# Four GNN layers on one core: the ring's first gathers put ahead of the rest pass, half steps spread over all chunks in the second layer, 28 low blocks instead of 24 in the wide layer

## What is computed

```python
x = layernorm(x + gru(x, segment_sum(mlp([x[src], edge_attr]), dst)))         # L0
x = layernorm(x + relu(conv_both_directions(x) @ W.T + bias))                 # L1: edges and reversed edges
x = layernorm(x + prelu(conv(x @ W) + b))                                     # L2: edges
h = relu(conv_w(x @ W1) + b1)      # 128 -> 256                               # L3, with edge weights
h = relu(conv_w(h @ W2) + b2)      # 256 -> 256
x = layernorm(x + conv_w(h @ W3) + b3)                                        # 256 -> 128
# conv(h)[d] = sum over edges (s, d) of norm(s, d) * h[s], and the node itself
```

## Time and profile before

| | us |
|---|---|
| median of 3 runs | 4691.67 |
| lowest, highest | 4690.04, 4700.65 |
| the profiled execution: own time | 4686.37 |
| its span, first to last instruction | 4684.6 |

### The profile page before, as it was taken

The page is one execution under the profiler, slowest core; times in us unless marked ns, Lnnn a source line. Parts: engine busy times, 40 slices in busy tenths (PEclk is TensorE's granted clock), DMA queues, the critical chain, the costliest instruction groups (busy, mean ns, idle before and its releaser), DMA issues. The chain is left out here.

```text
span 4684.6 us, 82764 instructions
## 1 busy us (share of the span) xinstructions
PE 3824.4 (82%) x30767; PEld 2562.3 (55%) x30767; DVE 3060.0 (65%) x6135; ACT 1471.8 (31%) x3024; POOL 2818.3 (60%) x2361
## 2 busy tenths in 40 slices
PE   2788899999899823277779788699989989997998
PEld 2666788888788823233334444444554555554444
DVE  5898999999999858645553334356536666633665
ACT  0333565665666602100000000033314444421332
POOL 3567788888888500067740577377727666524774
PEclk6777999998999956688999899899999999998999
DMA  5344777777777721199986677599956555545997
GB/s 162 113 126 125 222 240 228 242 237 231 248 236 237 231 92 39 48 314 317 313 262 192 201 222 228 184 323 322 330 190 207 193 183 200 183 161 206 331 327 259
DMA packets 611991, 1019.31 MB, mean 218 GB/s; under 512 B 90372, under 2 KB 417056, under 8 KB 611208
## 3 DMA queue, kind: packets, MB, share of 16 engines
q1 hardware_dynamic: 475788, 773.72, 48.5%
q0 software_dynamic: 90848, 199.74, 14.5%
q10 hardware_dynamic: 44956, 40.55, 2.7%
HBM read 736.98 MB, written 276.75 MB: 216 GB/s over the span
## 5 line engine op out<-in xcount | busy, mean ns | idle before, releaser
L871 POOL DMA_INDIRECT x<-p_table,src_i x832 | 1210.0, 1454 | 395.8 <-issue 226.3
L1373 POOL DMA_INDIRECT rows_b<-x_table,low_src x552 | 589.9, 1069 | 213.3 <-issue 165.1
L1373 POOL DMA_INDIRECT rows_a<-h_table,low_src x412 | 446.5, 1084 | 236.0 <-issue 121.1
L853 ACT CAST st_cnt<-ps_mat 128x512 bf16<-128x512 f32 (+1 forms) x825 | 440.8, 590 | 444.5 <-PE ps_deg L768 396.4
L1443 PE MATMUL po_l3b<-mat_l3b,rows_b 128*128 128x512 f32 (+1 forms) x1372 | 562.8, 557 | 20.5 <-DMA mat_l3b<-weights_fwd 19.5
L1443 PE MATMUL po_l3a<-mat_l3a,rows_a 128*128 128x512 f32 (+1 forms) x882 | 376.5, 574 | 23.5 <-DMA mat_l3a<-weights_fwd 22.7
L1443 PE MATMUL po_l3c<-mat_l3c,rows_a 128*128 128x512 f32 (+1 forms) x882 | 375.1, 572 | 16.2 <-DMA mat_l3c<-weights_fwd 15.4
L1443 PE MATMUL po_l<-mat_l,rows_a 128*128 128x512 bf16 (+1 forms) x1323 | 303.3, 384 | 87.8 <-DVE mat_l L1682 86.9
L783 PE MATMUL ps_mat<-rows_a,hot_s 128*128 128x128 bf16 x4851 | 363.5, 227 | 8.6
L1443 PEld LDWEIGHTS po_l3b<-mat_l3b,rows_b 128*128 128x128 f32 x1372 | 239.1, 194 | 237.9 <-issue 216.5
L598 DVE TENSOR_TENSOR rows_a<-rows_a,slots 128x1792 bf16<-128x1792 bf16 (+1 forms) x198 | 366.6, 1884 | 1.4
(11 more groups left out here) (407 smaller groups left out, 7663.0 us busy)
## 6 DMA issues: line engine op xcount, KB each, us to landing
weights_fwd<-st_wt SPq DMA_DIRECT2D x396, 256.0 KB
mat_l<-counts_fwd SPq DMA_DIRECT2D x112, 896.0 KB
mat_l3a<-weights_fwd SPq DMA_DIRECT2D x56, 1792.0 KB
mat_l3c<-weights_fwd SPq DMA_DIRECT2D x56, 1792.0 KB
counts_rev<-st_cnt SPq DMA_DIRECT2D x588, 128.0 KB
rev_l<-counts_rev SPq DMA_DIRECT2D x84, 896.0 KB
mat_l3b<-weights_fwd SPq DMA_DIRECT2D x42, 1792.0 KB
counts_fwd<-st_cnt SPq DMA_DIRECT2D x396, 128.0 KB
```

Source lines behind the costliest of these rows:

```text
L853: nc.scalar.copy(st_cnt[:, q, :, j * 2 * P:j * 2 * P + n_col], ps_mat[:, f % 3, :].rearrange("p (d c) -> p d c", d=2)[:, :, 0:n_col]).then ...
L871: pool.indirect_dma_start(ring[:, j % RING, t * FD:(t + 1) * FD], None, p_table, bass.IndirectOffsetOnAxis(src_i[:, j * TH + t:j * TH + t ...
L1373: pool.indirect_dma_start(ring[:, j % RL, t, :], None, table, bass.IndirectOffsetOnAxis(low_src[:, j * TH + t:j * TH + t + 1].bitcast(U32), 0)
```

## The change

1. On POOL the gathers of the first RL half steps (16 DMAs, 12 in l3b) stand ahead of the rest pass, in all five layers.
2. In l2 `usable` takes in all chunks, so the 69 half steps run to the last chunk.
3. LOWS is (16, 28): in l3b one dense group (4 blocks) becomes low. 6 dense groups and 120 half steps stand where 7 and 103 stood; 4 half steps in each of the chunks 7 to 36, where 2 or 3 stood in each of the chunks 7 to 43.
4. For room, `diag` has one buffer: `own_rows(f)` waits for `summed` f instead of f - 1. The tiles `hot2`, `edge1` and `row1` of L0's rest pass lie in the room of `x`.

```diff
-LOWS = (16, 24)
+LOWS = (16, 28)
...
-                hot2 = sb("hot2", [P, 3, P], F32, c2)
-                edge1 = sb("edge1", [ED + 1, P], F32, c2)
-                row1 = sb("row1", [P, FD], F32, c2)
+                hot2 = x_room[:, 0:3 * P].rearrange("p (q c) -> p q c", q=3)
+                edge1 = x_room[0:ED + 1, 3 * P:4 * P]
+                row1 = x_room[:, 4 * P:5 * P]
...
-            usable = sum(weights) - (0 if both else (CHKS - LATER[0] + 1) * weights[-1])
+            usable = sum(weights) - (0 if both or kind == "prelu" else (CHKS - LATER[0] + 1) * weights[-1])
...
-                diag = sb(f"diag_{name}", [P, 2, GB, P], F32, c)
+                diag = sb(f"diag_{name}", [P, GB, P], F32, c)
...
+                        def rest():
+                            rounds, tiles = rest_counts(pool)
...
+                            reg_loop(pool, rounds, a_round)
+                        def rows_of_step(j):
                             if j >= RL:
...
+                        for j in range(min(RL, low_js)):
+                            rows_of_step(j)
+                        rest()
+                        for j in range(RL, low_js):
+                            rows_of_step(j)
...
-                            if f >= 2:
-                                dve.wait_ge(summed, f - 1)
-                            mark = V.tensor_tensor(diag[:, f % 2, 0:nb, :], per_block(ident[:], nb),
+                            if f:
+                                dve.wait_ge(summed, f)
+                            mark = V.tensor_tensor(diag[:, 0:nb, :], per_block(ident[:], nb),
```

More of the change, by code:

```diff
@@ L1349, in _, with a_round, a_tile @@
                     def _(pool):
[L1350 to L1368, removed]
+                        def rest():
+                            rounds, tiles = rest_counts(pool)
+                            def a_round(v):
+                                def a_tile(t):
+                                    taken_by(pool, rest_go, 1)
+                                    pool.sem_inc(passed, 1)
+                                    for q in range(kinds):
+                                        at = kinds - 1 - q
+                                        pool.indirect_dma_start(
+                                            row2[:, q, :], None, table,
+                                            bass.IndirectOffsetOnAxis(rec_t[:, at:at + 1].bitcast(U32), 0)
+                                        ).then_inc(rest_rows, 16)
+                                    taken_gathered(pool, rest_rows, 16 * kinds)
+                                    pool.sem_inc(rest_got, 1)
+                                reg_loop(pool, tiles, a_tile)
+                            reg_loop(pool, rounds, a_round)
+                        def rows_of_step(j):
                             if j >= RL:
@@ L1461, in own_part @@
                                     rows = given[:, g * GB + d, k * P:(k + 1) * P] if exact else own[:, f % 2, d, :]
-                                    mm = nc.tensor.matmul(po[:, b, k, d * P:(d + 1) * P], rows, diag[:, f % 2, d, :],
+                                    mm = nc.tensor.matmul(po[:, b, k, d * P:(d + 1) * P], rows, diag[:, d, :],
                                                           start=alone, stop=(alone or d == nb - 1))
```

## The result

| | before | after |
|---|---|---|
| median, us (4 runs each) | 4691.35 | 4806.79 |
| lowest to highest | 4690.04 to 4700.65 | 4801.26 to 4809.82 |
| the profiled execution: own time, span | 4686.37, 4684.6 | 4807.55, 4805.8 |

The account below looks back on a forecast made before the run. POOL's gathers were taken to bound l2 and the changed l3b, where PE had set the end before. Terms 5 - 2 + 13 + 75 + 13 = +104 on 4686.4 gave 4790.4, stated as 4792 us; range 4720 to 4835.

Parts of the forecast that it names:

- l2: Second layer: the spread alone gains 14.5 us, the ring takes it back; -2 us (-6 to +8).
- l3b: Wide layer: POOL's 464 gathers at 1.40 us plus 60 us of waits set its length; +75 us (+3 to +132).
- Ring first: Start of each layer: gathers ahead delay the rest pass; l1 +5, l3a and l3c +13 us each.
- Rival C: Rest passes: the ring costs them nothing; l1, l3a, l3c 0, l2 -14, l3b +66, kernel 4738 us; chance 0.06.
- 60 in all: POOL's waits in l3b: 49 us at eight places, 4 for one lone `turn`, 1.5 each behind some five `conv`.
- eight places: l3b chunks 13, 16, 23, 25, 27, 30, 32, 34, with `turn` and `own_part` between half steps: 6.1 us each.
- six old places: Like places in l3b before the change: POOL waits of 6.7 to 10.1 us, going on 19 us after the half step.
- A: Wide layer: POOL's waits vanish; l3b +3 to +35, kernel 4718 to 4750 us; chance 0.15.
- B: Wide layer: POOL keeps pace below 1.2 us a gather, PE stays the bound; l3b -64, kernel 4652 us; chance 0.06.
- It waits for POOL by 100 to 150 us: Wide layer, chunks 7 to 36: PE needs 554 us itself and waits for POOL by 100 to 150 us.
- D: Wide layer: waits as before and 1.44 us a gather; l3b +110 to +132, kernel 4825 to 4860 us; chance 0.10.
- E: Wide layer: every DVE instruction of a half step blocks POOL; l3b +305, kernel 5020 us; chance 0.01.

Follow-up runs that it names:

- e2: Against the kernel before: only the room and the first RL half steps' gathers ahead of the rest pass; 4756.5 us, ratio 1.0106.
- e3: Against the kernel before: only the room and l2's half steps spread to its last chunk, rest pass first; 4686.96 us, ratio 0.9962.
- e4: Against the kernel before: only the room and 28 low blocks in l3b, rest pass first; 4780.99 us, ratio 1.0161.
- e9: The whole change again, unaltered, on another chip; 4814.18 us where the kernel before took 4697.08, ratio 1.0248.
- e12: Whole change, but ring behind the rest pass; in l3b finishing ahead of its chunk's half steps, which spread to the last chunk; 4664.20 us, 0.9918 of before.
- e10: Whole change with DVE's finishing ahead of the chunk's half steps in l3b, on e9's chip; 4775.78 us, ratio 1.0167 to before, 0.992 of e9.
- e1: Against the kernel before: only the room (one diag buffer, L0's rest tiles in the room of x); 4700.0 us, ratio 0.9996.
- e6: Same kernel as e10 (whole change, finishing first in l3b) on the chip where the kernel before took 5260 us; 5347.85 us, ratio 1.0155.

## Why the prediction was right

Slower by 2% was forecast, for the reasons that the runs show. 4792 was given, 4806.79 measured. The profiled execution's own time is 121.2 us longer, the sum said 104. The miss of 17 is made of +15.5 in l3b, +7.4 ahead of l1, +2.9 in l1 and -6.8 in l3c, the rest under 2 each; that some of these cancel is luck:

| term | predicted | measured | single part |
|---|---|---|---|
| up to l1 | 0 | +7.4 | |
| l1 | +5 | +7.9 | e2: +7.4 |
| l2 | -2 | -2.5 | e2: +13.5, e3: -11.7 |
| l3a | +13 | +11.7 | e2: +10.6 |
| l3b | +75 | +90.5 | e2: +15.9, e4: +77.0 |
| l3c | +13 | +6.2 (e9: +13.2) | e2: +12.3 |

- **Ring first** was right in mechanism. The rest's gathers came 20.8 us (l3a, l3c) and 15.2 us (l3b) after the start, where 22 and 17 were said; PE stood idle 15.2 to 17.9 us in the pass of l2, l3a and l3c, where 19 were said. In l1 the rest's gather came 8.4 us later and the layer took 7.4 to 7.9 longer: it got back 1 us at most of the 4 that were taken, which is its miss of 3 us. Rival C (the ring costs nothing) fell with e2.
- **l2** was right: gather 17 came 43.1 us after the layer's start, 43 was said. The spread alone was worth 11.7 to 13.3 (e3, e12), 14.5 was said; the ring took 13.5 back.
- **l3b**, counted as the prediction did. Step 4's gather came 11.0 us later, 8.3 was said. From there to the last gather 464 gathers took 724.4 us, 83.2 of it waits (80.8 for DVE's planes, and two pauses of 0.7 and 1.8): 641 without them or 1.382 each, where 1.40 was taken (650, so 9 too much, which hid a part of the next miss). The tail is as long as before (97.5 against 97.9).
- **The mis-sized term is "60 in all" for the waits: they were 83.** The eight places were named rightly: eight waits over 5.9 us, 66.8 in sum, 8.35 each against 6.1. The others came to 16 us where 11.5 was taken. The prediction took over from the six old places that POOL goes on 19 us after the half step before. At the eight new ones it was 21.7 on average (23.2 at the place shown). Two things grew. `turn` began 8.2 us after that half step instead of 6.6, since DVE came to `finish` later. And `turn` and `own_part` together took 5.2 us instead of 4.0, since PE ran at the lower clock in all eight; of the six old places three had that in part already (`turn` 1.93, 1.97 and 1.46 us), the second of the two shown among them. The prediction had noticed the clock in the rest pass and not here.
- **Rivals.** A said that POOL's waits vanish by themselves; they didn't, but with DVE's list turned (e10) they did, and l3b came to +43 over before, near A's +35. B (PE stays the bound) fell: the pace was 1.382 us a gather, waits left out. Its sum is wrong: (554 + 60) / 464 is 1.32, not 1.2 (554 alone gives 1.19). 1.382 is above both, but the margin was smaller than it looked. D's waits came half way, its 1.44 a gather did not. E fell by its size: the gathers were held by DVE (see the end), but each only to the end of one instruction, 0.14 us a gather.
- "POOL is the bound" was too simple. "It waits for POOL by 100 to 150 us" was right in sum (140 us of waits for DVE in the changed kernel), but 56 of these were waits for the finishing, which stood behind half steps that waited for gathers.
- The 7.4 us ahead of l1 are put down to scatter: with the room alone the time is unchanged (e1), and l1 began anywhere from 1958.5 (e3) to 1979.2 (e2) in kernels that do the same up to there.

## What to carry to other kernels

- Before work moves from a full engine to one nearly as full, fix the order on the engine between them. Here DVE's finishing stood behind waits for gathers; put first, it gave 41 us. That giving PE's work away pays after that is not shown: l3b was 841 us then, still above the 798 of 24 blocks, and e12 gained by the spread as well.
- Prefetches issued ahead of something that all engines wait for delay it (16 gathers of 1.25 us put the rest's gather of l3a 14 us later) and give little back if the ring was full in time anyway: each layer lost 7 to 16 us in e2.
- In an ordered list, ask what stands behind the last step of the engine that sets the pace. Here 97 us of other work stood behind the last half step. Spread beside the gathers it made the tail 60 us shorter and the stretch ahead of it 15 longer.

## What the hardware showed

- **The clock turns a wait into a longer one.** After 5.7 us without work PE's next two pieces ran at 1.2 GHz (1.97 and 3.62 us for 1.04 and 1.95). With the finishing first all `turn` ran at full clock.
- **DVE instructions that read two tensors in SBUF hold a gather until they end.** In l3b of the changed kernel, behind step 4, 192 gathers that began while DVE did nothing took 0.945 us on average, 116 that began inside `off_high` (L1657) 1.00, and 100 that began inside `last_plane` (L1663) 1.53, up to 1.97. Every one of the 157 that took over 0.96 ended 0.81 to 0.83 us after the end of the DVE instruction in which it began, whatever its own start: 97 inside `last_plane`, 51 inside `off_high`, the others inside L1649, L1679 and L1704. Rows of e10:

```profile
3748.29 1.23 DVE L1663 TENSOR_TENSOR split_l3b<-rows_a,split_l3b 128x1024 bf16<-128x1024 f32 x1 [0.91 <-ACT split_l3b L1565]
3748.36 1.97 POOL L1374 DMA_INDIRECT rows_a<-h_table,low_src  x1 [0.30 <-issue]
...
3750.03 1.23 DVE L1699 TENSOR_TENSOR sums_l3b<-po_l3b,left_l3b 128x1024 f32<-128x1024 f32 x1 [0.52 <-PE po_l3b L1470]
3750.64 0.95 POOL L1374 DMA_INDIRECT rows_a<-h_table,low_src  x1 [0.30 <-issue]
3751.29 1.22 DVE L1704 TENSOR_TENSOR sums_l3b<-sums_l3b,acc_l3b 128x1024 f32<-128x1024 f32 x1
3751.89 1.45 POOL L1374 DMA_INDIRECT rows_a<-h_table,low_src  x1 [0.30 <-issue]
```

  The first and the third gather are held (they end 0.81 and 0.83 us after DVE's instruction), the second is not: L1699 reads one of its two tensors (`po_l3b`) from PSUM. Of the 51 gathers of e10 that began inside such an instruction (L1672, L1699, L1723) none took over 0.96. `off_high` costs little only because each of its four instructions is short (0.48 us). The mean of the 464 gathers is 1.089, 0.14 over 0.945 and 67 us in sum; with 0.30 of issue that is the pace of 1.38 or 1.39. The Trainium skill ("SBUF — State Buffer", SBUF: two separate sides, the "DVE blocks DMA" trap) says that some DVE instructions lock GpSimd out of the port it writes descriptors through. The rows agree, and show that here the hold ends with the one instruction.
- **Chips differ.** One took 12% longer for the same kernel before (5260 us), and with DVE's order changed, which was worth 0.8% on another chip, seven long POOL waits were left there (e6).
